# One gather and one scatter in turn on GpSimd, with TensorE waiting for the gather itself

## What is computed

```python
x = L0_attn_x                                   # 16 x 256 x 128
xn = _layernorm(x, axis=-1)
# attention: q, k = elu(xn @ W.T) + 1; kv = sum over n of k v; q @ kv / (q @ sum of k + EPS), then @ Wo.T
# experts:
aff = x @ centroids.T
assign = jnp.argmax(aff, axis=1)                # one of 8 experts for each token
alpha = jax.nn.sigmoid(...)                     # of the best affinity
h = _layernorm(xs, ln_g[e], ln_b[e])
h = jax.nn.relu(h @ w1[e].T + b1[e])
ye = xs + h @ w2[e].T + b2[e]
out_sorted = alpha * y + (1.0 - alpha) * xs
x = x + attention(xn) + experts(xn)
```

## Time and profile before

| | us |
|---|---|
| Time, median of 3 runs | 194.03 |
| lowest and highest | 192.61, 195.37 |
| span of the profiled execution, first to last instruction | 230.4 |
| PE busy in that span | 158.5 |
| DVE busy | 131.6 |
| POOL busy | 116.5 |
| ACT busy | 103.0 |

### The profile page before, as it was taken

How to read it: one execution, slowest core, us unless ns; L and a number is a source line. 1 busy time by engine, 2 the same in 40 slices (tenths; PEclk the granted TensorE clock), 3 DMA queues, 4 the chain that set the end, 5 groups by cost and what they waited for, 6 DMA issues and landing times.

```text
span 230.4 us, 4618 instructions
## 1 busy us (share of the span) xinstructions
PE 158.5 (69%) x1113; PEld 144.8 (63%) x1114; DVE 131.6 (57%) x430; ACT 103.0 (45%) x325; POOL 116.5 (51%) x129
## 2 busy tenths in 40 slices
PE   0063678590695525966889979989682899997730
PEld 0053568590694425956878879878672799975620
DVE  3599994699921303632545564536371276637992
ACT  2026374885074204343255536363540456546660
POOL 7052675286057740447645655646377355351360
PEclk9999977999569795899799999999999799999995
DMA  5996321920001210011111111211201010003947
GB/s 142 267 318 235 91 73 31 337 110 0 0 16 46 58 46 0 26 34 40 47 23 45 46 36 34 46 34 38 30 19 42 27 34 24 12 28 107 289 132 202
DMA packets 20910, 18.22 MB, mean 79 GB/s; under 512 B 2464, under 2 KB 19363, under 8 KB 20640
## 3 DMA queue, kind: packets, MB, share of 16 engines
q1 hardware_dynamic: 18400, 13.40, 19.9%
q0 software_dynamic: 2496, 4.66, 7.9%
HBM read 11.76 MB, written 6.75 MB: 80 GB/s over the span
## 4 chain that ended last, share of the span: by engine, by line
PE 38%; DVE 27%; another core or an unknown queue 14%; issue 7%; ACT 5%; DMA 2%; ACTq 1%; DVEq 1%; SPq 1%
PE bank L643 11%; PE bank L635 10%; PE bank L594 4%; DVE lane_hot L854 4%; DVE base L998 3%; PE bank L553 3%; DMA x<-in_x 2%; PE bank L623 2%; DVE stats L711 2%; ACT hT L469 2%; DVE zscale L757 2%; PE bank L545 2%; PE bank L606 2%; PE bank L527 2%
## 5 line engine op out<-in xcount | busy, mean ns | idle before, releaser
L469 ACT ACTIVATE hT<-bank,b 128x128 f32<-128x128 f32 x156 | 44.3, 368 | 43.2 <-PE bank L635 26.7
L343 POOL DMA_INDIRECT y_rows<-xn_and_y_tiles,scatter_at x39 | 39.4, 1009 | 35.3 <-DVE xn_and_y_tiles L943 22.9
L331 POOL DMA_INDIRECT rows<-z_rows,gather_at x39 | 37.8, 970 | 25.9 <-PE bank L629 17.6
L643 PE MATMUL bank<-w,hT 128*128 x312 | 44.4, 288 | 3.6 <-ACT hT L469 3.1
L635 PE MATMUL bank<-zT,w_now 128*128 128x128 f32 x312 | 45.3, 292 | 2.2 <-DVE w_now L939 2.0
L635 PEld LDWEIGHTS bank<-zT,w_now 128*128 128x128 f32 x312 | 40.9, 205 | 5.6 <-issue 3.4
L643 PEld LDWEIGHTS bank<-w,hT 128*128 128x128 f32 x312 | 40.5, 203 | 5.1 <-issue 5.1
L936 DVE TENSOR_SCALAR zT<-bank,ln_g,ln_b 128x128 f32<-128x128 f32 x39 | 16.0, 409 | 19.7 <-remote 12.9
L943 DVE TENSOR_TENSOR xn_and_y_tiles<-bank,b 128x128 f32 (+1 forms) x39 | 11.3, 290 | 20.4 <-PE bank L643 13.0
L518 PE MATMUL bank<-ident,xn_and_y_tiles 128*128 128x128 f32 x32 | 7.6, 391 | 21.2 <-DVE xn_and_y_tiles L764 21.2
L623 PE MATMUL bank<-wo,headsT 128*128 128x128 f32 x64 | 11.4, 304 | 12.9 <-DVE base L930 4.6
(11 more groups left out here) (123 smaller groups left out, 273.4 us busy)
## 6 DMA issues: line engine op xcount, KB each, us to landing
w<-in_w1T SPq DMA_DIRECT2D x1, 2048.0 KB, 9.7
z_rows<-z SPq DMA_DIRECT2D x4, 512.0 KB, 3.4
w<-in_w2T SPq DMA_DIRECT2D x1, 2048.0 KB, 9.0
z<-y_rows SPq DMA_DIRECT2D x8, 256.0 KB, 4.9
x<-in_x SPq DMA_DIRECT2D x3, 512.0 KB, 6.9
out<-base SPq DMA_DIRECT2D x6, 256.0 KB, 2.8
rows<-z_rows,gather_at POOLq DMA_INDIRECT x39
y_rows<-xn_and_y_tiles,scatter_at POOLq DMA_INDIRECT x39
```

The source lines that it names most:

```text
L331: g.indirect_dma_start(out=rows[:, s % RING, :], out_offset=None, in_=z_dram, in_offset=bass.IndirectOffsetOnAxis(ap=gather_at[:, s:s + 1] ...
L343: g.indirect_dma_start(out=y_dram, out_offset=bass.IndirectOffsetOnAxis(ap=scatter_at[:, s:s + 1], axis=0), in_=y_rows[:, s, :], in_offset ...
L469: last = a.activation(hT[:, par, c * P:(c + 1) * P], bank[2 + par][:, c * P:(c + 1) * P], ACT.Relu, bias=b1[:, c, bass.ds(e, 1)])
L643: last = t_.matmul(bank[6 + par][:, 0:D], hT[:, par, c * P:(c + 1) * P], w2[:, bass.ds(e * (FC * D) + c * D, D)], start=(c == 0), stop=(c ...
```

## The change

- `gather(s)` waits for the transpose of slot `s-4` instead of `s-12` (`wait_for(pool, zt_done, s - AHEAD + 1)`). The ring still has 12 buffers, of which gathers now run four ahead.
- `landed` and the counter `gathered` are gone. PE's `turn_rows` waits for `gather_in[place % AHEAD]` itself; inside the loop the value comes from the loop's turn.
- POOL issues one gather and one scatter in turn: `scatter(s-7)` behind `gather(s)` (`BEHIND` = 7). So 32 scatters stand among the gathers and 7 behind them, where it was 18 and 21.
- The mask of `kv_all` moves from behind the last gather to between `gather(7)` and `scatter(0)`.

```diff
+    BEHIND = 7
...
             def gather(s):
-                wait_for(pool, zt_done, s - RING + 1)
+                wait_for(pool, zt_done, s - AHEAD + 1)
                 g.indirect_dma_start(
...
-            def landed(s):
-                pool.wait_ge(gather_in[s % AHEAD], 16 * (s // AHEAD + 1))
-                pool.sem_inc(gathered, 1)
...
-            sent = 0
-            for s in range(NSLOT):
-                if s >= AHEAD:
-                    landed(s - AHEAD)
-                gather(s)
-
-                if s > RING and s % 3:
-                    scatter(sent)
-                    sent += 1
-            for s in range(NSLOT - AHEAD, NSLOT):
-                landed(s)
-
-            pool.wait_ge(kv_copied, NB)
-            g.tensor_tensor(kv_all[:, NB1:NB, :], kv_all[:, NB1:NB, :], head_mask[:, :].unsqueeze(1).to_broadcast([P, NB - NB1, KVW]),
-                            ALU.mult).then_inc(last_kv_ready, 1)
-            for s in range(sent, NSLOT):
-                scatter(s)
+            for s in range(NSLOT + BEHIND):
+                if s < NSLOT:
+                    gather(s)
+                if s == BEHIND:
+                    pool.wait_ge(kv_copied, NB)
+                    g.tensor_tensor(kv_all[:, NB1:NB, :], kv_all[:, NB1:NB, :], head_mask[:, :].unsqueeze(1).to_broadcast([P, NB - NB1, KVW]),
+                                    ALU.mult).then_inc(last_kv_ready, 1)
+                if s >= BEHIND:
+                    scatter(s - BEHIND)
...
-            def turn_rows(s, par, place):
-                pe.wait_ge(gathered, s + 1)
+            def turn_rows(s, par, place, turn_of_ring=None):
+                pe.wait_ge(gather_in[place % AHEAD], (s // AHEAD + 1) * 16 if isinstance(s, int) else turn_of_ring * 16)
...
-                    turn_rows(s + 1, 1 - par, (place + 1) % RING)
+                    turn_rows(s + 1, 1 - par, (place + 1) % RING, k * (RING // AHEAD) + ((n + 3) // AHEAD + 1))
```

More of the change, by code:

```diff
@@ L201, in linear_attention_and_routed_experts @@
         base_ready = sem("base_ready")
-        gathered, zt_done, zt_ready, w1_ready, h_done, h_ready, y_done, y_ready = (
-            sem(n) for n in ("gathered", "zt_done", "zt_ready", "w1_ready", "h_done", "h_ready", "y_done", "y_ready"))
+        zt_done, zt_ready, w1_ready, h_done, h_ready, y_done, y_ready = (
+            sem(n) for n in ("zt_done", "zt_ready", "w1_ready", "h_done", "h_ready", "y_done", "y_ready"))
         scaled, pool_added, dve_added = sem("scaled"), sem("pool_added"), sem("dve_added")
```

## The result

The changed kernel takes 197.89 us, median of 4 runs (196.79 to 198.4), against 193.95 for the kernel before: ratio 1.021, interval 1.016 to 1.026. Forecast were 197.3 us, +3.3 us and +1.7%; measured are +3.94 us, +2.0%.

A forecast was written before the change was run, and what follows sets the result against it. PE's work, with gaps, bounds the kernel; afterwards POOL's 2.60 us per slot would. 194.03 us plus 3.05 (later last transpose) and about 0.3 (late landings), taken as 3.3, gave 197.3; range 192.8 to 201.0.

The forecast's parts named there:

- The base: Starting time: profiled span 230.4 us less 26.2 and 11.3 us of stops, 192.9; stops belong to the profiled execution.
- Gather(8): POOL issues slot 8's gather 5.3 us after T3, the time at which PE transposes slot 3.
- POOL's period: One gather and one scatter per slot on POOL take 2.60 us against PE's 2.34, so POOL becomes slower.
- Landing: A gather's rows are there for PE 2.7 us after its issue, bounds 2.2 and 3.7.
- PE afterwards: Changed kernel: PE waits a little per slot from about slot 22; last transpose 86.0 us after slot 3's.
- PE before: Kernel before: 35 slots at 2.34 us plus the mask's 1.05 put the last transpose 82.95 us after slot 3's.
- Afterwards that collision falls where PE has slack.: Mask beside DVE's copy, which cost PE 1.05 us before, costs nothing afterwards: PE has up to 3.7 us slack.
- The end: Last scatter ends 8.6 us after the last transpose, y 0.7 us later; the loads absorb it, else up to 0.7.
- POOL wasn't late: Kernel before, last scatters: POOL's own work would end at T3 + 89.4 us, against 90.9 for the actual end.
- A: Rival: PE still sets the pace in the slots, no change, 193 to 195 us; chance 0.27.
- B: Rival: DVE copies lock out POOL's issues, period 3.02 us if fully, 203 to 211 us; chance 0.09.
- C: Rival: faster by over 2%, below 190.2 us, early scatters letting the final loads come sooner; chance 0.03.

The follow-up runs named there:

- `before_again`: The kernel before, profiled once more with no edit: 194.01 us, without stops.
- experiments 5 to 9: Changed kernel with different padding rows, a memset per slot, no edit, or twelve gathers stored up; kernel before with no relay and early mask. All with stops.
- experiments 1 to 4: Kernel before again, 194.01 us; changed kernel with mask earlier, 195.56, or gathers free to the ring, 195.61; kernel before with gathers four ahead, 206.45.
- experiment 7: The changed kernel once more with no edit, under stops: 234.59 us beside 233.99 for the kernel before.
- `mask_early`: Changed kernel with the mask between gather(6) and gather(7): 195.56 us, 1.007 of before.
- experiment 4: Kernel before with gathers four slots ahead and PE waiting on them itself, POOL's old list kept: 206.45 us in one execution.
- experiment 2: The run `mask_early`: changed kernel with the mask one gather earlier, 195.56 us, 1.007 of before.
- `after_again`: The run of experiment 7: changed kernel with no edit, under stops, 234.59 us beside 233.99 for the kernel before.
- experiment 5: Changed kernel with padding places gathering different rows, run twice under stops: 236.76 us beside 233.82 for the kernel before, and 226.66 beside 232.32.
- `lead7`: Changed kernel with gathers free to run as far ahead as the ring's 12 slots: 195.61 us, 1.012 of before.
- experiment 6: Changed kernel with one more GpSimd memset per slot, run twice under stops: 233.27 us beside 233.82 for the kernel before, and 227.8 beside 232.32.
- `lead12_mask_early`: Changed kernel with twelve gathers before the first scatter, gathers free to the ring, mask behind gather(7): 0.994 and 1.000 of before, under stops.

## Why the prediction was right, step by step

- **The base.** Right in size, wrong in reason. The stop-free sum gave 192.9; the span of `before_again` is 192.2, and about 1.8 us lie around a span (198.03 against 196.2). But the stops don't "belong to the profiled execution". In the runs of experiments 5 to 9, on three chips, the times of all executions are those with stops, and on the chip of experiments 1 to 4 none are. Whether they belong to the chip or to the time at which it ran isn't shown, since no chip was used twice. It was luck that the runs shown had none: where they are, the same working would have forecast a loss that experiment 7 doesn't show.
- **Gather(8).** Predicted T3 + 5.3, measured 5.1.
- **POOL's period.** Predicted 2.60, measured 2.63: 0.9 us more over 30. Issues that start inside a DVE copy take up to 1.11 for a gather. `mask_early` has 2.61.
- **Landing.** The term of the sum that was most off. 2.7 is right for a full slot (2.5 in the median), but the end hangs on slot 37, whose rows were there 3.65 after the issue, and the last transpose starts 3.78 after its own gather's. That is the upper bound of 3.7, which I put aside "since in the longer case a scatter had been queued". The reason was the padding: the wait of the earlier trace rows was for slot 38's gather too, the same 128 reads of one row.
- **PE afterwards.** T3 + 87.73 instead of 86.0: + 0.9 for the period, + 1.1 for the landing, - 0.2 for gather(8).
- **PE before.** 83.98 instead of 82.95. PE's own pace is 83.30 / 35 = 2.38 (experiment 4, with 0.4 us of the mask's in it), not 2.34: in that trace four slots take 9.3 to 9.45 us, but 9.7 to 9.8 where a turn of the loop ends among them (slots 15 and 27), and the four that I read had no such place. The mask cost 0.66 in `before_again`, not 1.05. So the end before moved by + 1.0 and the end afterwards by + 1.7, and the difference of 3.05 became 3.75. The sum was close by luck: misses on both sides had one sign.
- **"Afterwards that collision falls where PE has slack."** Half right. The copy of slot 4 took 1.96 us and PE waited 1.30. PE came 1.30 us later to every slot behind it, and with the pace of 2.38 that left it more to spare (an estimate: 13.4 - 5.1 - 2.5 = 5.8 us at slot 8 instead of 3.7, used up at 0.25 a slot by slot 31). So it ran dry only at slot 32, not at 22, and in three waits at padded slots, 2.2 us in all, not "a little in each slot". The collision didn't move the end: that hangs on POOL (experiment 2).
- **The end.** Predicted 0.7 us later for y, within what the loads have to spare; measured 7.90 after the last transpose against 8.04 in `before_again`, no later at all. The rows of the last slots came late by a us, which gave POOL time: its last scatter stood 0.67 us idle instead of 0.30. And "POOL wasn't late" before was wrong by its whole margin. The working has gather(38) at T3 + 56.7, held by a transpose that it counts 24 slots behind slot 3 (slot 26's, for which it waits, is 23 behind). Measured are T3 + 59.2, held by POOL's own list, and a last scatter that ends at T3 + 92.0, not 89.4, with no idle time behind the mask but the usual gaps.
- **Rivals.** A would have needed a mean pace of 2.43, and PE's is 2.38: nearer than it looked. With stops POOL does wait for PE, as A says (experiment 7). B: copies under POOL's issues are longer (0.5 to 0.7 us instead of 0.42 in eight of 39), but POOL's period grew by 0.03 and not by 0.42. C did not happen.
- **The profiled span** "hardly changes, because the stops cover it": 230.4 and 228.2 (`after_again`) under stops, 192.2 and 196.2 without. That holds like for like.

## What to carry to other kernels

Add up what the issuing engine has to do per turn of a loop and put it beside the pace of the engine it feeds; when the first is larger, only a store of early transfers hides it, and a change that shortens the store or adds an idle wait ahead of it brings the difference out at the end of the loop. Read the landing of each transfer and not only their median: what decided the end here were slots that are mostly padding. An operation that is added to make a period longer must be seen to do so in the trace before the time says anything. Before a profile is used to price an edit, find out whether the runs have the profile's stops; the same edit cost 2% without them, and with them no difference could be seen.

## What the runs showed of the hardware that was not expected

- A gather of 128 times the same DRAM row lands 3.5 to 3.6 us after its issue, one of 128 different rows as a rule after 2.4 to 2.8 (changed kernel); its packets end 2.7 us after the issue, and 1.9 with different rows (slot 37, experiment 5). In `mask_early` and `lead7` the eight padded slots land after 3.0 to 3.6 too, but two and four of the others also take 3.0 or more.
- Between two indirect DMAs GpSimd has a gap of 0.30 us, and a memset of 128x1 (0.11 to 0.30 us) fits into it: the period stays at 2.59 to 2.62 us (experiment 6).
- In the traces of experiments 5 to 9 engines stop with no releaser in the trace: in `after_again` ScalarE 6 times for up to 4.6 us ahead of the copy of `headsT`, 24.7 us in all, in the kernels with twelve gathers ahead mostly at other instructions (5 times for up to 5.9 us ahead of the relu in `lead12_mask_early`). The traces of the changed kernel and of experiments 1 to 4 have none. Where the stops come from stays open.
- GpSimd's multiplication of 128x864 and the DVE copy of 128x512 float32 don't run together: the copy took 1.55 us beside it and 1.96 in the changed kernel, instead of 0.42, and ended 0.28 and 0.29 us behind the multiplication. Moved to a stretch without copies, the 2.02 us are free. The Trainium skill, "SBUF — State Buffer", section "Who interferes with whom", has this as an exclusive lock, and the trace agrees; for indirect DMAs a share of the issue alone was held back, at most 0.28 us (1.233 against a median of 0.953).
